# An attention and expert layer on eight cores: plain loads of V's weights, expert tiles started beside attention, expert rows stored by token

## The chip, the cores and the metric

The kernel runs on all 8 cores of one Trainium2 chip. Every core works on one of eight batch entries (2048 tokens of 1024 features) and holds its own copy of all weights; the cores exchange nothing. A core has TensorE (PE in the rows), VectorE (DVE), ScalarE (ACT), GpSimd (POOL) and SyncE (SP), and 16 DMA engines that all queues share. The metric is the device time in microseconds of the slowest core.

## What is computed

The reference, cut to what matters (x is one batch entry, B = 8, T = 2048, D = 1024):

```
xn = layernorm(x)
q, k, v = split(xn @ w_qkv.T + b_qkv)             # 16 heads of 64
q = silu(q);  k = softmax(k, over the tokens)
out = layernorm(q @ (k.T @ v)) * g + b            # per head: kv is 64x64
gate = sigmoid((xn @ w_g1.T + b_g1) @ w_g2.T + b_g2)
attn = (out * gate) @ w_out.T + b_out
logits = xn @ Wr.T                                # 8 experts
w = softmax(top_2(logits));  C = 769 rows at most per expert
ffn[t] = sum over the token's 2 experts of w[t,k] * (xn[t] @ We[expert])
y = x + attn + ffn
```

A token that arrives at a full expert is dropped there, and its row from that expert is zero. An expert gets 512 rows on average.

## The kernel before

All engines are programmed by hand: the code appends instructions to five lists (`PE`, `DV`, `AC`, `SP`, `GP`), each executed strictly in order, and `after` adds the semaphore waits. So what stands in a list behind a waiting instruction waits too. `move` appends a DMA to a list; `when` puts the instructions of a block between a branch and its target, on the engines named. Five weight slots of 2 MB in bfloat16 (`wring` 0 to 2 and the two halves of `wlate`) hold V's, K's, Q's, the eight experts' and the output weights one after another.

1. **Head** (`for s in range(NT + 2)`, line 484 on). Each of 16 tiles of 128 tokens is loaded from `x_tm` in float32, normalised (`h_stats`, `h_root`, `h_norm`), rounded to bfloat16 (`h_hi`), stored as `xn_d`, turned on TensorE into `xnT` (`h_trans`), multiplied by V's weights in two halves of 512 columns (`h_v`), and given to the router (`h_router`). V's weights arrive as two DMAs from GpSimd's queue that round from float32 on the way (`w_half`).
2. **K** (`for j in range(NJ + 2)`). 32 steps of projection, exponential, transpose and the product with V. The list `route` feeds the router's small VectorE work in beside them. At the start, nine stores of zeros clear the part of the expert results `eo_d` that experts may leave unwritten.
3. **Attention** (`for b in range(NB + 2)`, 8 units `u` each). Block b projects Q for 512 tokens (`q_proj`), block b+1 computes the attention rows and their statistics (`a_out`, `a_norm`), block b+2 the gate and the product (`a_gate`, `a_z`). So the last two blocks have no projection, and the last one has gates and products alone.
4. **Experts** (`for J in range(NJT)`, NJT = 40). Every expert has five tiles of 128 rows: four always, the fifth under a branch on the expert's count (`SURE` = 4). A sixth and seventh are under further branches (`m_rare`). Tile J: GpSimd gathers 128 rows of `xn_d` (`m_load`, six ahead), TensorE turns them and ScalarE copies them out (`m_trans`), 16 matmuls of 512 columns follow, VectorE scales one half by the token's weight and ScalarE the other (`m_rows`), and SP stores 256 KB to `eo_d`, ordered by expert and slot. Three buffers `eo` hold results on their way out. The branches stand on all five engines. GpSimd also loads the later weights by quarters (`next_quarter`), and SP the tiles of x for the last stage (`o_base`).
5. **Output** (`o_rows`, `o_proj`, `o_add`). For each of 16 token tiles GpSimd gathers the two expert rows of every token from `eo_d`, TensorE does 16 matmuls of the output projection and adds both gathered rows with four matmuls by the identity into the same banks, VectorE adds x and the bias, and ScalarE's queue stores y.

Lines to know: 298 is every matmul, 302 every transpose, 306 every activation, 313 ScalarE's and 314 VectorE's copies, 321 a tensor by a scalar, 317 a tensor by a tensor, 902 the gather of experts' rows, 1023 the gather of results, 112 and 120 branches.

## Time and profile before

| | us |
|---|---|
| three runs, median (lowest, highest) | 614.62 (614.15, 662.0) |
| the profiled execution, its own time | 614.46 |
| its span on the slowest core, core 0 | 612.9 |
| spans of the eight cores | 600.8 to 612.9 |
| head, to the first K projection | 0 to 118 |
| K | 118 to 222 |
| attention, blocks 0 to 3 | 222 to 313 |
| attention, blocks 4 and 5 | 313 to 350 |
| experts | 350 to 537 |
| output | 537 to 613 |

TensorE is busy for 486.9 us of the span (79%), VectorE for 267.4, ScalarE for 220.4 and GpSimd for 157.9. The chain that ended last is TensorE for 46% and DMA for 23%. The stages follow each other on TensorE, so an interval saved in one is saved at the end only if the next stage's inputs are there. A matmul row can be missing from the trace, so counts such as x15 in place of x16 mean nothing.

### The profile page before, as it was taken

Reading aid. Unit: us, or ns where it says so; the run is one execution under the profiler, and the core shown is the slowest. Engines: PE = TensorE matmul, PEld = TensorE weight load, DVE = VectorE, ACT = ScalarE, POOL = GpSimd, SP = SyncE. Lnnn points to the kernel's source line nnn. Section 1 sums busy time; section 2 is a strip of 40 time slices with the busy share of each in tenths; the row PEclk is TensorE's granted clock in tenths of the full one; section 3 lists DMA queues with packets and bytes.
Section 4 is the critical chain, followed back from the end, with each engine's and each line's share of the span. In section 5 each row is a group of like instructions: output and inputs, shape, how many; then the busy total and the mean of one; then the engine's idle time right before and its main releaser. Section 6 shows DMA issues by size and latency. Waiting matters only on the chain.

```text
span 612.9 us, 9186 instructions; the slowest of 8 cores (600.8 to 612.9 us)
## 1 busy us (share of the span) xinstructions
PE 486.9 (79%) x3080; PEld 247.7 (40%) x3136; DVE 267.4 (44%) x609; ACT 220.4 (36%) x339; POOL 157.9 (26%) x148
## 2 busy tenths in 40 slices
PE   0269999887679789997855598958778898899996
PEld 0135555444334454443422254424434444444442
DVE  1536766367885631465657611011110111315555
ACT  0414435253345423554543435334434354300000
POOL 3214445300090000100011425413322110055551
PEclk9979999999989989999965589999998998989999
DMA  9916991999990074000063349999999985158886
GB/s 162 223 52 193 194 249 55 169 221 211 214 185 15 1 110 65 0 1 2 0 90 49 103 124 207 254 225 193 215 173 198 215 264 157 69 153 235 247 240 240
DMA packets 40054, 91.54 MB, mean 149 GB/s; under 512 B 5632, under 2 KB 7808, under 8 KB 40000
## 3 DMA queue, kind: packets, MB, share of 16 engines
q0 software_dynamic: 21024, 44.39, 43.7%
q1 hardware_dynamic: 16528, 38.04, 18.8%
q10 hardware_dynamic: 2448, 8.42, 3.5%
q8 instruction: 30, 0.49, 0.4%
q14 instruction: 24, 0.20, 0.1%
HBM read 87.77 MB, written 28.57 MB: 190 GB/s over the span
## 4 chain that ended last, share of the span: by engine, by line
PE 46%; DMA 23%; DVE 12%; issue 11%; ACT 6%; DVEq 1%; POOL 0%; ACTq 0%; PEldq 0%; SPq 0%; POOLq 0%
PE PS L298 42%; DMA stage<-xn_d,tabs 9%; DMA eo_d<-stage 7%; DMA wr<-wv_t 5%; PE PS L302 4%; ACT stage L306 3%; DVE bst L816 3%; DVE nm L683 2%; DMA wlate<-x_tm 2%; ACT vq L306 1%; DVE stage L322 1%; ACT e_sb L313 1%; DVE nb L322 1%; DVE stage L317 1%; DVEq L100 0%
## 5 line engine op out<-in xcount | busy, mean ns | idle before, releaser
L298 PE MATMUL PS<-wr,xnt 128*128 128x512 bf16 x493 | 118.9, 391 | 17.0 <-DMA wr<-wv_t 9.4
L298 PE MATMUL PS<-xnt,wr 128*128 128x512 bf16 x492 | 118.4, 382 | 1.8 <-ACT vq L306 0.8
L321 DVE TENSOR_SCALAR stage<-PS,wslot_f 128x512 bf16<-128x512 f32 x36 | 26.9, 751 | 155.0 <-PE PS L298 111.7
L298 PEld LDWEIGHTS PS<-wr,xnt 128*128 128x128 bf16 x512 | 49.9, 100 | 77.7 <-issue 23.9
L302 PE MATMUL PS<-ident_sb,stage 128*128 128x128 bf16 x576 | 43.7, 226 | 46.9 <-DVE stage L314 21.9
L298 PE MATMUL PS<-wr,stage 128*128 128x512 bf16 x280 | 70.4, 405 | 5.3 <-ACT stage L313 4.2
L298 PEld LDWEIGHTS PS<-xnt,wr 128*128 128x128 bf16 x512 | 48.1, 98 | 50.4 <-issue 3.3
L298 PE MATMUL PS<-wlate,stage 128*128 128x512 bf16 x279 | 64.9, 381 | 1.2 <-ACT stage L313 0.8
L902 POOL DMA_INDIRECT stage<-xn_d,tabs x40 | 39.0, 974 | 94.8 <-PE PS L302 82.3
L302 PEld LDWEIGHTS PS<-ident_sb,stage 128*128 128x128 bf16 x576 | 37.8, 101 | 62.0 <-issue 52.8
L306 ACT ACTIVATE stage<-PS,wslot_f 128x512 bf16<-128x512 f32 x36 | 24.8, 688 | 83.6 <-PE PS L298 58.3
L1023 POOL DMA_INDIRECT stage<-eo_d,slot x32 | 35.1, 1096 | 63.8 <-DMA eo_d<-stage 37.7
L317 POOL TENSOR_TENSOR stage<-stage 128x1024 bf16<-128x1024 f32 x16 | 34.0, 2124 | 65.3 <-DVE stage L314 62.3
L298 PEld LDWEIGHTS PS<-wr,stage 128*128 128x128 bf16 x288 | 29.1, 104 | 39.8 <-issue 13.4
L313 ACT COPY stage<-PS 128x1024 bf16<-128x1024 bf16 x40 | 40.2, 1007 | 9.8 <-PE PS L302 9.7
L308 ACT ACTIVATE eT<-PS,nb 128x512 bf16<-128x512 f32 x32 | 22.0, 688 | 51.3 <-DVE nb L322 25.2
L298 PEld LDWEIGHTS PS<-wlate,stage 128*128 128x128 bf16 x288 | 27.6, 99 | 30.8 <-issue 1.5
L317 POOL TENSOR_TENSOR rs<-sd,half_sb 128x1 f32<-128x1 f32 x16 | 8.8, 549 | 108.6 <-DVE sd L321 108.6
L306 ACT ACTIVATE stage<-wlate,nmr,rs 128x1024 f32<-128x1024 f32 x16 | 19.8, 1240 | 41.2 <-DVE nmr L322 35.0
L326 DVE SCALAR_TENSOR_TENSOR xnt<-stage 128x512 bf16<-128x512 f32 x32 | 22.2, 693 | 20.2 <-ACT stage L306 16.6
L306 ACT ACTIVATE vq<-PS,nmr,rs 128x1024 bf16<-128x1024 f32 x16 | 19.3, 1204 | 30.9 <-DVE nmr L322 30.9
L683 DVE TENSOR_REDUCE nm<-PS 128x1 f32<-128x512 f32 x32 | 22.1, 690 | 16.0 <-PE PS L298 16.0
(138 smaller groups left out, 540.1 us busy)
## 6 DMA issues: line engine op xcount, KB each, us to landing
wlate<-x_tm SPq DMA_DIRECT2D x20, 512.0 KB, 6.6
eo_d<-stage SPq DMA_DIRECT2D x37, 256.0 KB, 8.5
eo_d<-stage SPq DMA_DIRECT2D x8, 768.0 KB, 37.1
wr<-we POOLq DMA_DIRECT2D x3, 2048.0 KB, 19.3
xn_d<-stage SPq DMA_DIRECT2D x16, 256.0 KB, 6.6
wlate<-we POOLq DMA_DIRECT2D x2, 2048.0 KB, 49.8
vq<-x_tm SPq DMA_DIRECT2D x8, 512.0 KB, 13.6
wlate<-we POOLq DMA_DIRECT2D x8, 512.0 KB, 24.1
```

What stands on the lines that cost most here:

```text
L298: return PE.run(lambda e: e.matmul(out, l, r, start=start, stop=stop), *toks, sig=sig)
L302: return PE.run(lambda e: e.transpose(out, in_, ident[:]), *toks, sig=sig)
L306: return AC.run(lambda e: e.activation(out, in_, func, bias=bias, scale=scale), *toks)
L308: return AC.run(lambda e: e.activation(out, in_, func, bias=bias, scale=scale, accum_out=acc), *toks)
L313: return AC.run(lambda e: e.copy(out, in_), *toks)
L317: return lane.run(lambda e: e.tensor_tensor(out, a, b, op), *toks)
L321: return lane.run(lambda e: e.tensor_scalar(out, a, s1, None, op0=op0), *toks)
L326: return lane.run(lambda e: e.scalar_tensor_tensor(out, a, s, b, op0=op0, op1=op1), *toks)
L683: a = DV.run(lambda e: e.tensor_reduce(nm[:, j:j + 1], bank[bk], AX.X, ALU.max, negate=True), p)
L816: m = DV.run(lambda e, h=h, bk=bk: e.bn_stats(bst[:, s, h, :], bank[bk]), p)
L902: GP.steps.append((lambda e: e.indirect_dma_start(out=out, out_offset=None, in_=xn_d, in_offset=bass.IndirectOffsetOnAxis(ap=tabs[:, col:c ...
L1023: GP.steps.append((lambda e: e.indirect_dma_start(out=dst, out_offset=None, in_=eo_d, in_offset=bass.IndirectOffsetOnAxis(ap=slot[:, col:c ...
```

## The change

- V's weights are loaded as float32 by plain DMAs, in eight pieces, from ScalarE's and SP's queues, and rounded by VectorE and ScalarE. The second half of the V product runs three tiles behind the first, so the head's loop has two steps more.
- The clearing of `eo_d` now covers the 4096 token rows (8 MB in place of 6.5), in four stores that are released in K's steps 20 to 23.
- A sixth weight slot lies in `stage`: expert 4's weights are loaded right after K, and from there each expert's weights, and the output weights, are loaded one expert earlier.
- Tiles 0 to 6 of the experts' 40 run in attention's blocks 4 and 5, one per two units (`m_beside`, `m_step`). Gathers run eight ahead in place of six, and there are six result buffers in place of three.
- GpSimd stores a tile's rows by token (row 2*token + choice of `eo_d`) with an indirect DMA (`m_put`) after each of all 40 tiles. Slots without a token go to spare rows.
- The output stage reads both rows of a token with one plain DMA of 512 KB per token tile from SP. One row is added on VectorE, the other by two matmuls with the identity.
- The branches stand on TensorE and VectorE alone (and on GpSimd for the sixth and seventh tile). ScalarE and SP have none.
- x's tiles for the output are loaded later, during experts 4 to 7, and their bias is added during experts 5 to 7 and before the output.

The diff, cut to its core:

```diff
-        wsl = [w[:] for w in wring] + [wlate[:, 0:HC * D], wlate[:, HC * D:2 * HC * D]]
+        wsl = [w[:] for w in wring] + [wlate[:, 0:HC * D], wlate[:, HC * D:2 * HC * D],
+                                       stage[:, 0:HC * D]]
...
-            x_tok = {0: load_x(0), 1: load_x(1)}
-            x_tok[2] = load_x(2, x_tok[0])
-            x_tok[3] = load_x(3, x_tok[1])
+            x_tok = {0: load_x(0)}
+            x_tok[1] = load_x(1, x_tok[0])
...
+            def wv_load(lane, h, q, *toks):
+                wv_in[h, q] = lane.move(
+                    counter(f"c_wv{h}{q}"), wvf[h][:, 2 * q:2 * q + 2, :],
+                    wv_t.rearrange("(c p) o -> p c o", p=128)[:, 2 * q:2 * q + 2,
+                                                              512 * h:512 * (h + 1)], *toks)
+            def wv_cast(lane, h, c):
+                t_wv[h, c] = tcopy(lane, wv3[0][:, c, 512 * h:512 * (h + 1)], wvf[h][:, c, :],
+                                   wv_in[h, c // 2])
+            for q in range(4):
+                wv_load(AC, 0, q)
+            act(warm[:], eps_sb[:], AF.Sqrt, t_const)
+            x_tok[2] = load_x(2, wv_in[0, 3])
+            wv_load(SP, 1, 0)
+            wv_load(SP, 1, 1)
+            x_tok[3] = load_x(3)
+            wv_load(SP, 1, 2)
+            wv_load(SP, 1, 3)
...
+                    late["wk"] = w_load(1, wk_t, stat[t], *[t_wv[1, c] for c in range(HC)])
...
-            for s in range(NT + 2):
+            wv_cast(AC, 0, 3)
+            for s in range(NT + 4):
...
+                if s in (2, 3):
+                    for c in range(4 * s - 8, 4 * s - 4):
+                        wv_cast(AC, 1, c)
...
+                v0 = h_v(s - 1, 0) if 1 <= s <= NT else None
+                v1 = h_v(s - 4, 1) if s >= 4 else None
...
+                b = ts(DV, idle[:], tok_f[:], 0.0, ALU.is_lt, None, None, a)
+                a = tt(DV, tok_i, tok_f[:], idle[:], ALU.add, b)
+                tk["tab"] = DV.run(lambda e: e.tensor_single_scalar(
+                    tabs[:], tok_i, 1, ALU.arith_shift_right), a)
+                b = tt(DV, idle[:], idle[:], spare[:], ALU.mult, a)
+                tk["dst"] = tt(DV, dtab[:], tok_f[:], idle[:], ALU.add, b)
...
-            wslot = {e: (3, 4, 0, 1, 2)[e % 5] for e in range(E)}
+            wslot = {e: (3, 4, 0, 1, 5, 2)[e % 6] for e in range(E)}
...
-            for e in range(E):
-                t_ez = SP.move(
-                    c_ez, eo_d[e * SE + 128 * SURE:(e + 1) * SE, :].rearrange(
-                        "(k p) d -> p k d", p=128),
-                    nil.rearrange("p (o d) -> p o d", o=1).broadcast_to([128, ET - SURE, D]),
-                    t_nil, stat[NT - 1])
-            t_ez = SP.move(c_ez, eo_d[NSLOT:NSLOT + 128, :], nil)
+            def clear_rows():
+                for q in range(4):
+                    tk["clear"] = SP.move(
+                        c_ez, eo_d[q * T // 2:(q + 1) * T // 2, :].rearrange(
+                            "(k p) d -> p k d", p=128),
+                        nil.rearrange("p (o d) -> p o d", o=1).broadcast_to([128, 8, D]),
+                        t_nil, kv_pe[20 + q])
...
+            load_we(4, 5, tk["hot_free"])
...
+            def a_pair(t):
+                return t % 2 if t < NT - 4 else 0
...
+            BESIDE = 7
...
+            def m_load(J):
+                xg_tok[J] = fetch_rows(c_xg[J % 8], xg[J % 8], (J // XE) * ET + J % XE, tk["tab"],
+                                       xtr.get(J - 8), ao_pe[NT - 5 if J % 8 < 4 else NT - 1],
+                                       *[xd_tok[t] for t in range(NT - 4, NT)])
...
+            def put_rows(done, src, col, *toks):
+                GP.after(*toks)
+                GP.steps.append((lambda e: e.indirect_dma_start(
+                    out=eo_d, out_offset=bass.IndirectOffsetOnAxis(ap=dtab[:, col:col + 1], axis=0),
+                    in_=src, in_offset=None), done, 16))
+                return done.up(16)
...
+                    if h == 0 or i >= SURE:
+                        a = ts(DV, half, bank[bk], w, ALU.mult, None, None, p, tk["tw"], *free)
+                    else:
+                        a = act(half, bank[bk], AF.Copy, p, tk["tw"], *free, scale=w)
...
+            def m_out(J):
+                pair = 1 if J < 3 else J % 2 if J < BESIDE else J % 3
+                mo_pe[J], out_tok[J] = m_rows(J // XE, J % XE, pair, xgT[J % 3], xgt_tok[J],
+                                              eo[J % 6], [st_tok.get(J - 6), ntr[NB - 2] if
+                                                          2 <= J < 6 else None, t_ez])
+            def m_put(J):
+                st_tok[J] = put_rows(c_eo[J % 6], eo[J % 6], (J // XE) * ET + J % XE, tk["dst"],
+                                     t_ez, *out_tok[J])
...
+            def m_step(J):
+                e, i = J // XE, J % XE
+                if J + 1 < NJT:
+                    m_trans(J + 1)
+                if i < SURE:
+                    m_out(J)
+                else:
+                    with where(e, 128 * SURE, PE, DV):
+                        m_out(J)
+                        pair = (J + 1) % 2 if J < BESIDE else (J + 1) % 3
+                        with where(e, 128 * (SURE + 1), PE, DV, GP):
+                            m_rare(e, SURE + 1, pair)
+                            with where(e, 128 * (SURE + 2), PE, DV, GP):
+                                m_rare(e, SURE + 2, pair)
+                    freed[e] = PE.now()
+                    if e + 6 < E:
+                        t_we[e + 6] = quarters(wslot[e], we[e + 6:e + 7, :, :].rearrange(
+                            "e a b -> (e a) b"), freed[e])
+                    elif e + 6 == E:
+                        wo["slot"] = wslot[e]
+                        wo["tok"] = quarters(wslot[e], wo_t, freed[e])
+                m_put(J)
+                if J + 8 < NJT:
+                    m_load(J + 8)
+                next_quarter()
+                for k in range(4):
+                    if J // XE == 4 + k and i < 4:
+                        o_base(4 * k + i, freed[3 + k])
+                    if J // XE == 5 + k and i < 4:
+                        o_bias(4 * k + i)
+            def m_beside(b, u):
+                if b == 0 and u == 0:
+                    for lane in (PE, DV, GP):
+                        lane.after(tk["cnt"])
+                        lane.read(cnt_i)
+                if b == 0 and u == 7:
+                    for J in range(4, 8):
+                        m_load(J)
+                if b == 0 and u == 1:
+                    m_trans(0)
+                if u % 2 and b * 8 + u >= 3:
+                    m_step((b * 8 + u - 3) // 2)
...
+                    if b >= NB:
+                        m_beside(b - NB, u)
                 if b == NB - 1:
-                    load_we(4, 2, qfree[NB - 1])
+                    for J in range(4):
+                        m_load(J)
+                    t_we[5] = quarters(2, we[5:6, :, :].rearrange("e a b -> (e a) b"),
+                                       qfree[NB - 1])
+                    next_quarter()
+                    next_quarter()
...
-                return p, SP.move(done, eo_d[e * SE + 128 * i:e * SE + 128 * (i + 1), :], out, a, b)
...
+            for J in range(BESIDE, NJT):
+                m_step(J)
...
-                ga[t] = gather(c_ga[i], ga_sb[i], t, t_rows, tk["si"], t_ez, rows_pe.get(t - 4),
-                               *t_st)
-                gb[t] = gather(c_gb[i], gb_sb[i], NT + t)
...
+                r_tok[t] = SP.move(c_rows[t % 4], rows_sb[t % 4], eo_d[256 * t:256 * (t + 1), :]
+                                   .rearrange("(p k) d -> p (k d)", k=2),
+                                   rows_pe.get(t - 4), r0_tok.get(t - 4), *t_st)
...
-                for k, (rows, got) in enumerate(((ga_sb[s], ga[t]), (gb_sb[s], gb[t]))):
-                    for h in range(2):
-                        p = mm(bank[2 * s + h], ident[:], rows[:, 512 * h:512 * (h + 1)], False,
-                               k == 1, got, sig=(k == 1))
+                r0_tok[t] = tt(DV, xb[t], rows_sb[s][:, 0:D], xb[t], ALU.add, r_tok[t], xo_tok[t])
+                for h in range(2):
+                    p = mm(bank[2 * s + h], ident[:],
+                           rows_sb[s][:, D + 512 * h:D + 512 * (h + 1)], False, True, r_tok[t],
+                           sig=(h == 1))
                 rows_pe[t] = p
-                a = tt(DV, xb[t], PS[:, 1024 * s:1024 * (s + 1)], xb[t], ALU.add,
-                       p, xo_tok[t])
+                a = tt(DV, xb[t], PS[:, 1024 * s:1024 * (s + 1)], xb[t], ALU.add, p, r0_tok[t])
...
+            for t in range(NT - 4, NT):
+                o_bias(t)
```

The order on TensorE in attention's block 4, one pair of units, before (gate: `gh,wg_sb`; turned attention rows: `ident_sb,vq`; attention product: `kv_sb,vq`):

```order
250 L298 MATMUL PS<-kv_sb,vq 128x128 x8
251 L298 MATMUL PS<-gh,wg_sb 128x512
252 L302 MATMUL PS<-ident_sb,vq 128x128 x4
253 L298 MATMUL PS<-gh,wg_sb 128x512
254 L302 MATMUL PS<-ident_sb,vq 128x128 x4
```

and the same place now, a pair later (the transposes x12 are four of attention and eight of the next expert tile):

```order
256 L310 MATMUL PS<-gh,wg_sb 128x512
257 L314 MATMUL PS<-ident_sb,vq 128x128 x4
258 L310 MATMUL PS<-kv_sb,vq 128x128 x8
259 L310 MATMUL PS<-gh,wg_sb 128x512
260 L314 MATMUL PS<-ident_sb,vq 128x128 x12
261 L310 MATMUL PS<-wlate,stage 128x512 x16
262 L310 MATMUL PS<-gh,wg_sb 128x512
```

A tile's 16 matmuls now stand between two gates, so the next gate and all that waits for it come behind them.

The order on ScalarE in blocks 4 and 5, before (`vq<-PS,nmr,rs`: the attention rows normalised; `stage<-PS,bg_sb`: the gate):

```order
183 L306 ACTIVATE vq<-PS,nmr,rs 128x1024
184 L306 ACTIVATE stage<-PS,bg_sb 128x512 x2
185 L306 ACTIVATE vq<-PS,nmr,rs 128x1024
186 L306 ACTIVATE stage<-PS,bg_sb 128x512 x2
187 L306 ACTIVATE vq<-PS,nmr,rs 128x1024
```

and now:

```order
187 L318 ACTIVATE stage<-PS,bg_sb 128x512 x2
188 L318 ACTIVATE vq<-PS,nmr,rs 128x1024
189 L325 COPY stage<-PS 128x1024
190 L318 ACTIVATE stage<-PS,wslot_f 128x512
191 L318 ACTIVATE stage<-PS,bg_sb 128x512 x2
192 L318 ACTIVATE vq<-PS,nmr,rs 128x1024
```

Between the normalisation and the next two gates stand a copy (the next tile turned) and half a tile's scaling.

GpSimd at the end of expert 0 and the start of expert 1's rows, before (`xn_d` is the gather, `we` a quarter of a weight; the branches belong to the sixth and seventh tile):

```order
33 L902 DMA stage<-xn_d,tabs 128x1024
34 L105 UNCONDITIONAL_BRANCH x3
35 L100 UNCONDITIONAL_BRANCH
36 L902 DMA stage<-xn_d,tabs 128x1024
37 L75 DMA wlate<-we 128x2x1024
```

and now:

```order
55 L108 UNCONDITIONAL_BRANCH
56 L111 UNCONDITIONAL_BRANCH
57 L965 DMA eo_d<-vq,dtab 11264x1024
58 L940 DMA vq<-xn_d,tabs 128x1024
59 L78 DMA wlate<-we 128x2x1024
```

The store of results has moved from SP's queue to GpSimd's, where it stands ahead of the next gather and quarter.

## Rows read from the trace of the kernel before

**Rows 1.** windows by stage: each engine's busy us (instructions), granted clock, DMA share, GB/s.

```profile
0.00:118.00 118.00, 81.36 (x756) 48.02 (x771) 59.63 (x139) 40.12 (x65) 44.88 (x37) 0.97 0.72 161
...
313.00:350.00 37.00, 20.98 (x111) 10.15 (x108) 25.10 (x52) 16.11 (x21) 8.41 (x10) 0.50 0.54 96
350.00:537.00 187.00, 153.11 (x882) 77.38 (x899) 31.15 (x42) 76.57 (x88) 45.10 (x50) 0.94 0.84 188
537.00:613.00 76.00, 70.29 (x314) 31.46 (x318) 34.69 (x30) 0.00 (x0) 35.08 (x32) 0.97 0.74 225
```

**Rows 2.** timeline, head: start us, us, engine, line, operation, tile, count, idle before.

```profile
24.76 3.57 PE L298 MATMUL PS<-wr,xnt 128*128 128x512 bf16 x8 [1.88 <-DMA wr<-wv_t]
...
35.83 3.37 PE L298 MATMUL PS<-wr,xnt 128*128 128x512 bf16 x8 [7.50 <-DMA wr<-wv_t]
```

**Rows 3.** chain of waits in the head: start us, us, what.

```profile
100.75 0.89 PE PS L302 x16
...
105.87 0.89 PE PS L302 x16
```

**Rows 4.** timeline, attention's last two blocks.

```profile
325.80 1.20 ACT L306 ACTIVATE vq<-PS,nmr,rs 128x1024 bf16<-128x1024 f32 x1 [2.65 <-DVE nmr L322]
...
331.74 1.20 ACT L306 ACTIVATE vq<-PS,nmr,rs 128x1024 bf16<-128x1024 f32 x1 [2.65 <-DVE nmr L322]
...
346.55 0.69 ACT L306 ACTIVATE stage<-PS,bg_sb 128x512 f32<-128x512 f32 x1 [0.88 <-PE PS L298]
...
348.12 0.69 ACT L306 ACTIVATE stage<-PS,bg_sb 128x512 f32<-128x512 f32 x1 [0.88 <-PE PS L298]
```

**Rows 5.** timeline, experts' tiles, ScalarE and TensorE.

```profile
491.61 0.61 PE L302 MATMUL PS<-ident_sb,stage 128*128 128x128 bf16 x8 [0.75 <-PEq L112]
...
503.31 0.61 PE L302 MATMUL PS<-ident_sb,stage 128*128 128x128 bf16 x8
503.63 0.69 ACT L306 ACTIVATE stage<-PS,wslot_f 128x512 bf16<-128x512 f32 x1 [2.31 <-PE PS L298]
...
504.21 1.00 ACT L313 COPY stage<-PS 128x1024 bf16<-128x1024 bf16 x1
...
507.21 0.61 PE L302 MATMUL PS<-ident_sb,stage 128*128 128x128 bf16 x8
...
513.62 1.01 PE L302 MATMUL PS<-ident_sb,stage 128*128 128x128 bf16 x8 [2.35 <-ACTq L112]
```

**Rows 6.** waits of TensorE in the experts: us in total, times, longest.

```profile
PE PS L302 <- DMA stage<-xn_d,tabs: 13.4, 8, 4.1
PE PS L302 <- ACTq L112: 7.8, 4, 2.4
PE PS L298 <- ACT stage L313: 4.9, 3, 2.3
PE PS L298 <- ACTq L112: 3.2, 2, 2.4
```

**Rows 7.** DMA issues in the experts: count, KB each, median us to landing.

```profile
eo_d<-stage SPq DMA_DIRECT2D x36, 256.0 KB, 8.4
...
stage<-xn_d,tabs POOLq DMA_INDIRECT x34, 20.3
```

**Rows 8.** loads and stores of xn_d, issue to landing.

```profile
DMA to landing us min/median/max: 2.0/10.1/33.8
```

**Rows 9.** DMA queues, 218 to 243 us, one weight load: packets, MB, share.

```profile
q0 software_dynamic: 1040, 2.10, 61.2%
```

**Rows 10.** DMA queues, 341 to 354 us, six gathers.

```profile
q0 software_dynamic: 480, 1.57, 46.9%
```

**Rows 11.** DMA queues, 512 to 533 us, plain stores and loads.

```profile
q1 hardware_dynamic: 940, 2.21, 31.0%
```

**Rows 12.** timeline, output stage.

```profile
601.40 3.62 PE L298 MATMUL PS<-wr,xnt 128*128 128x512 bf16 x15
601.74 1.23 DVE L317 TENSOR_TENSOR wlate<-PS,wlate 128x1024 f32<-128x1024 f32 x1 [1.96 <-PE PS L298]
```

357 lines of the change are left out of this document (161 added, 196 removed).

## The prediction, made before the changed kernel ran

> **What bounds the kernel now.** I read the windows by stage first, to see which stage is full and which is not. In the output stage TensorE is busy for 70.3 of 76 us, in the experts for 153.1 of 187, and in attention's last two blocks for 21.0 of 37 at a granted clock of 0.50, the lower level of 1.2 GHz [rows 1]. The first is bound by TensorE's work, the other two by something else.
>
> Then the timelines, for the distance between equal events. A full tile of the head costs 5.12 us (100.75 to 105.87, [rows 3]), back to back, so the head is TensorE's once V's weights are there; they are late: the first half ends a wait at 24.76 us and the second at 35.83 [rows 2]. In block 4 one normalisation follows another after 5.94 us, in block 5 one gate another after 1.57 us [rows 4]. An undisturbed expert tile costs 3.90 us (503.31 to 507.21, [rows 5]), 16 matmuls of 512 columns and eight transposes. A wide matmul takes about 0.22 us there (70.3 us for 314 in the output, [rows 1]). Then the waits of TensorE in the experts: 13.4 us for gathered rows, 4.9 for ScalarE's copy of them, and 11.0 (7.8 + 3.2) for ScalarE's sequencer at a branch [rows 6]; one such wait is 2.35 us, where TensorE's own branch costs 0.75 [rows 5]. So the experts lose time to transfers and to branches of another engine.
>
> **The change, part by part.** All times are against the profiled execution (614.46 us, span 612.9), which stands 0.2 us from the median of the three runs.
>
> Head: until the pipeline can run with both halves (step 4) five tiles of x and all of V's weights must land, 2.6 + 4.2 MB. At full share the head's DMAs moved 161 / 0.72 = 224 GB/s [rows 1]: 30 us. The nearest plain transfers took 31.0% of 21 us for 2.21 MB, 2.9 us per MB [rows 11]: 20 us. I take 30, since all 16 engines also wait for memory there. Done by then are three half products (3 x 1.7 us) and some 3 us of transposes and routing; left are 16 x 5.12 - 8 = 74 us. The first K projection comes at 104 instead of 118: **-14**. Bounds: -20 (second half usable at 24), -6 (at 38). The 16 roundings lie beside it: VectorE is busy for 60 and ScalarE for 40 of 118 us [rows 1].
>
> K and blocks 0 to 3: five small VectorE operations fewer, more zeros later and one weight earlier, where no DMA ends a wait of TensorE: **0**. The zeros must only land before block 2 writes over their source.
>
> Blocks 4 and 5: the loop of 5.94 us runs through VectorE's statistics, GpSimd's power, ScalarE's normalisation and the next gate. ScalarE now has a copy of 1.00 and a scaling of 0.69 us [rows 5] between the normalisation and that gate: 5.94 + 1.69 + 0.2 for two more starts = 7.8, three times, and once the copy alone: +6.6. In block 5 a pair of gates takes 3.14. Now the tile's 3.90, then its scaling 0.69, a gate's activation 0.69, and about 1.0 for the second gate, its transposes and the handovers, follow each other on TensorE: 6.3, four times: +12.6. I add 1 for matmuls that still start at the lower clock: **+20** for seven tiles that cost 27.3 at least where they stood. The eight register reads move with their cost. GpSimd has a store, a gather and a quarter per step, about 1 us each, in a step of 6.3 to 7.8, and the power is asked for behind them; if they take over 4 us, the next statistics wait.
>
> Experts: before, 350 to 537 less the register reads, about 184 us, for 36 computed tiles (36 x 3.90 = 140) and 44 of loss. After, 29 computed tiles are left on this core: 113. Four skipped ones cost a turn and a branch, 1.2 each: 5. Seven branches on TensorE at 0.75: 5. ScalarE's 11.0 go. The DMA's demand from the end of block 3 is four weights at 61.2% of 25 us = 15.3 [rows 9], 40 gathers at 46.9% of 13 us / 6 = 1.0 [rows 10], 40 stores, and 16 tiles of x at 1.5 (0.52 MB by [rows 11]). A store by index isn't in the trace. As a plain store it is 0.77 [rows 11]; as a gather 1.0 (I take this one, it is the same queue and the same number of rows); at worst one row packet as slow as under the weights' load, 15.3 / 2 MB x 0.26 = 1.9. Sum: 61 + 41 + 41 + 24 = 167 us in the 185 until the experts end (203 with the worst). While the quarters run, five tiles ask for 4 x 3.8 + 5 x 2.0 = 25 us in 20.5, so a backlog of about 10 to 15 us builds up. That is less than the lead of the gathers (eight tiles, 31 us) and of the buffers (six, 23 us). I leave 6 us for what slips through. 113 + 5 + 5 + 6 = 129, against 184: **-55**. Bounds: -61 (no waits left), -35 (the worst store, DMA bound at 203).
>
> Output: 32 matmuls by the identity go, 32 x 0.22 = 7.0. TensorE stays the bound: VectorE has two additions of 1.23 us [rows 12] in a tile of 3.9 us. DMA moves 1.05 MB per tile, 270 GB/s, where it now moves 225 at share 0.74 [rows 1]. The first rows wait for the last store by index; three projections (10.4 us) cover it: 1 us late. **-6**.
>
> Sum: -14 + 20 - 55 - 6 = -55, so 614.5 becomes **559**.
>
> **One rule against the change.** Stores from SP's queue landed after 8.4 us in the experts, the gathers of GpSimd's queue after 20.3 in the same stretch [rows 7]. The Trainium skill, DMA: Bandwidth & Descriptors, section Queues, rings and completion order, says that each DMA engine takes turns between the queue rows it has work for, while a row's own descriptors are consumed in order. By that rule a result store that leaves SP's row queues behind every weight quarter and gather, whatever its own price; the trace agrees (20.3 against 8.4). By bytes alone the sum would keep 8.4 us and no risk; by the rule the landing is 20 us and more, and the six buffers are needed. Rival 3 is what it gives at worst.
>
> **The rivals.** (1) As forecast: 0.62. Its own range is 543 to 573, from the bounds of head and experts.
>
> (2) The tiles beside attention run at the lower clock. For: it stood at 0.50 all through blocks 4 and 5 [rows 1]. Against: 3.5 us of wide matmuls in a step of 6.3 to 7.8 is a new kind of work there, and the experts' mean is 0.94 with 18% of idle time [rows 1]. Seven tiles at half speed cost 3.45 more each: +24, 583. Chance 0.12.
>
> (3) Slower than before: result stores land too late. A tile may write its buffer when the store six tiles back has landed. With a landing time L a tile then costs (L + 1) / 6 us, which decides from L = 22.4 on. The 20.3 is a median; the slowest gather took 33.8 [rows 8]. If 33 steps went at L = 33.8, a tile would cost 5.8 instead of 3.9: +63, 622. From L = 32 on the whole gain is gone. Against: the output weights are loaded by tile 17, and the plain stores leave SP's queue, so congestion covers half the stage. Chance 0.06.
>
> (4) The same shortage in a mild form: stores at the worst price and L near 26, +0.6 us per tile or the DMA bound of 203: +16 to +20, 575 to 579. Chance 0.14.
>
> (5) Nearly all expert waits vanish and V's weights come in 20 us: 541 to 545. Chance 0.06.
>
> **How the numbers follow.** The likeliest case gives 559. The range of 8 in 10 reaches from 540 (just under case 5) to 592 (cases 2 and 4 with some of the bounds on top), and leaves out case 3 and the sums of several mishaps. Within 2% of the time before, about what a measurement of this kernel tells from no change, is 602 to 627: cases 2 and 4 together, or case 3 in part, 0.06. Slower by more than 2%, the rest of case 3: 0.05. Faster by over 2%: 0.89.
>
> **What would show it.** Right: the first K projection near 104 us, ScalarE without table loads between experts' tiles, steps of about 7.8 us in block 4 and 6.3 in block 5 with the clock at its upper level, tiles of 3.90 us afterwards with under 10 us of waits for DMAs, and an output stage with tiles of 3.9 us. Wrong: the second half's first product after 38 us; steps over 9 us beside attention, with idle time ended by GpSimd or a gather; VectorE or ScalarE waiting for the stores of `eo_d` (the buffers); or TensorE waiting for rows of `eo_d` in the output.

## The result: faster by 4.6%, about half of what was forecast

The changed kernel took 0.954 of the time of the kernel before (95% interval 0.947 to 0.962). Its profiled execution took 586.6 us (span 584.9, core 0), against 614.5 (span 612.9). The forecast was 559 us, within 540 to 592; so the range held, but the likeliest case did not come. In a later comparison the same kernel stood at 0.951 (0.945 to 0.958). In some executions the cores of one die run several per cent slower, whatever the kernel, and all comparisons here leave those out.

The windows of the changed kernel, core 0, cut at its own stages (columns as in [rows 1]): head, K, blocks 0 to 3, blocks 4 and 5 with the seven tiles beside them, the other 33 expert steps, output:

```profile
0.00:112.00 112.00, 83.23 (x768) 48.87 (x769) 63.77 (x145) 46.25 (x77) 41.73 (x34) 0.95 0.76 191
112.00:217.00 105.00, 84.36 (x578) 44.41 (x577) 71.97 (x240) 43.62 (x107) 17.59 (x7) 0.93 0.73 150
217.00:307.00 90.00, 80.31 (x468) 37.34 (x466) 44.76 (x108) 44.44 (x60) 8.81 (x15) 1.00 0.31 50
307.00:367.00 60.00, 40.37 (x240) 20.82 (x240) 28.51 (x56) 25.35 (x32) 26.42 (x27) 0.77 0.53 121
367.00:514.00 147.00, 129.41 (x765) 65.27 (x764) 41.70 (x50) 50.02 (x61) 68.50 (x72) 0.94 0.84 207
514.00:585.00 71.00, 62.32 (x288) 28.11 (x288) 42.44 (x36) 0.00 (x0) 1.76 (x1) 0.97 0.71 241
```

| stage, core 0 | forecast change | measured change |
|---|---|---|
| head, to the first K projection | -14 | -6 |
| K and blocks 0 to 3 | 0 | 0 |
| blocks 4 and 5, now with seven tiles | +20 | +23 |
| experts | -55 | -40 |
| output | -6 | -5 |
| sum | -55 | -28 |

Two terms carry most of the miss of 27 us: 8 us in the head, 15 in the experts. The waits of TensorE in the experts of the changed kernel (367 to 520 us) answer to [rows 6]:

```profile
PE PS L314 <- DMA vq<-xn_d,tabs: 11.2, 3, 4.8
PE PS L314 <- DVEq L115: 2.4, 2, 1.2
PE PS L310 <- DVEq L115: 1.2, 1, 1.2
PE PS L310 <- ACT stage L325: 1.1, 2, 0.6
```

ScalarE's sequencer is gone from the list. The gathers cost nearly as much as before (13.4), but in three waits close together. The timeline of TensorE shows them; tiles before and behind this stretch are 3.90 us apart:

```profile
423.66 3.62 PE L310 MATMUL PS<-stage 128*128 128x512 bf16 x16
427.11 0.61 PE L314 MATMUL PS<-ident_sb,vq 128*128 128x128 bf16 x8
427.56 3.62 PE L310 MATMUL PS<-stage 128*128 128x512 bf16 x16
435.19 1.01 PE L314 MATMUL PS<-ident_sb,vq 128*128 128x128 bf16 x8 [4.02 <-DMA vq<-xn_d,tabs]
436.00 6.03 PE L310 MATMUL PS<-stage 128*128 128x512 bf16 x16
444.41 1.01 PE L314 MATMUL PS<-ident_sb,vq 128*128 128x128 bf16 x8 [2.37 <-DMA vq<-xn_d,tabs]
450.20 1.01 PE L314 MATMUL PS<-ident_sb,vq 128*128 128x128 bf16 x8 [4.78 <-DMA vq<-xn_d,tabs]
451.00 5.37 PE L310 MATMUL PS<-wr,stage 128*128 128x512 bf16 x16
456.65 3.62 PE L310 MATMUL PS<-wr,stage 128*128 128x512 bf16 x16
```

From 427.56 to 456.65 there are 29.1 us, where three steps of 3.90 and a skipped tile (the transposes at 444.41, without a product) take 13.6 in an undisturbed stretch. The 15.5 us between them are the experts' whole miss. Some 4 us of it are two groups of matmuls at a lower granted clock (6.03 and 5.37 us instead of 3.62) behind the waits. All three waits of TensorE name a gather. VectorE waits there too, for a free buffer, that is for a result store six tiles back:

```profile
441.52 0.75 DVE L333 TENSOR_SCALAR vq<-PS,wslot_f 128x512 bf16<-128x512 f32 x1 [9.13 <-DMA eo_d<-vq,dtab]
```

Windows of the same kernel around the stall:

```profile
370.00:380.00 10.00, 9.60 (x63) 4.95 (x60) 2.06 (x3) 3.87 (x6) 5.54 (x6) 1.00 0.69 137
380.00:430.00 50.00, 47.03 (x292) 24.19 (x293) 9.01 (x12) 19.87 (x24) 32.97 (x35) 1.00 1.03 212
430.00:455.00 25.00, 13.83 (x57) 6.38 (x56) 1.70 (x3) 4.41 (x5) 6.86 (x7) 0.66 1.01 264
455.00:514.00 59.00, 55.95 (x335) 27.98 (x333) 26.90 (x30) 20.18 (x25) 20.51 (x21) 1.00 0.64 195
```

The next-to-last column is what to read: the DMA engines are full from 380 to 455 us, and at 0.64 afterwards. The stall comes at the end of a full stretch, not at its beginning.

The first of the three waits can be followed from its gather, the one of tile 24 (tiles counted from 0; the row is GpSimd issuing it):

```profile
412.70 0.97 POOL L940 DMA_INDIRECT vq<-xn_d,tabs  x1 [0.30 <-issue]
```

TensorE was free for these rows at 431.17, 18.5 us later, and got them at 435.19. The changed kernel issues a gather eight tiles ahead, but that is not a lead of eight tiles: gather J+8 stands behind the store of tile J in GpSimd's list, and its transposes stand ahead of the matmuls of tile J+7 in TensorE's. Six tiles lie between. In an undisturbed stretch that is 21.3 us (the gather of tile 35 leaves at 467.08, its transposes start at 488.41: six tiles and a branch, less 3 us in which tile J is scaled and stored), and less where one of the six tiles is skipped, as here.

### The profile page after: what moved, and what is told of

Read it like the earlier page. It is cut to its first block, busy times and chain, and to the rows that moved or that the text cites. A ratio compares the mean times of both kernels' runs of the same rounds, so it can differ in the third digit from the quotient of the medians.

```text
span 584.9 us, 9174 instructions; the slowest of 8 cores (568.9 to 584.9 us)
## 1 busy us (share of the span) xinstructions
PE 480.0 (82%) x3104; PEld 244.8 (42%) x3104; DVE 293.1 (50%) x634; ACT 209.7 (36%) x337; POOL 164.8 (28%) x154
## 4 chain that ended last, share of the span: by engine, by line
PE 56%; DMA 13%; DVE 12%; issue 9%; ACT 6%; DVEq 1%; POOL 1%; ACTq 0%; SPq 0%; POOLq 0%; PEldq 0%
PE PS L310 51%; DMA vq<-xn_d,tabs 6%; PE PS L314 5%; DMA wlate<-x_tm 5%; DVE nm L735 3%; DMA wr<-wv_t 2%; ACT stage L318 2%; DVE bst L875 2%; ACT vq L318 1%; DVE stage L334 1%; ACT ek L325 1%; DVE nb L334 1%; DVE stage L329 1%; ACT stage L325 1%; DVE wlate L329 1%
## 5 line engine op out<-in xcount | busy, mean ns | idle before, releaser
L314 PE MATMUL PS<-ident_sb,vq 128*128 128x128 bf16 x448 | 40.4, 234 | 25.3 <-DMA vq<-xn_d,tabs 15.0
L333 DVE TENSOR_SCALAR vq<-PS,wslot_f 128x512 bf16<-128x512 f32 x28 | 21.0, 751 | 78.5 <-PE PS L310 69.3
L310 PE MATMUL PS<-wr,stage 128*128 128x512 bf16 x224 | 52.4, 388 | 0.6 <-ACT stage L325 0.6
L314 PEld LDWEIGHTS PS<-ident_sb,vq 128*128 128x128 bf16 x448 | 30.4, 104 | 43.1 <-issue 37.2
L940 POOL DMA_INDIRECT vq<-xn_d,tabs x40 | 40.3, 1008 | 12.2 <-issue 11.3
L965 POOL DMA_INDIRECT eo_d<-vq,dtab x26 | 27.9, 1073 | 55.5 <-ACT vq L318 31.2
L320 ACT ACTIVATE ek<-PS,nb 128x512 bf16<-128x512 f32 x32 | 22.0, 687 | 50.6 <-DVE nb L334 26.0
L314 PE MATMUL PS<-ident_sb,stage 128*128 128x128 bf16 x256 | 18.5, 229 | 17.9 <-DVE stage L326 13.8
L310 PEld LDWEIGHTS PS<-wr,stage 128*128 128x128 bf16 x224 | 21.8, 100 | 25.2 <-issue 2.9
L318 ACT ACTIVATE vq<-PS,wslot_f 128x512 bf16<-128x512 f32 x20 | 13.8, 688 | 51.0 <-PE PS L310 51.0
```

The source lines that it names most:

```text
L310: return PE.run(lambda e: e.matmul(out, l, r, start=start, stop=stop), *toks, sig=sig)
L314: return PE.run(lambda e: e.transpose(out, in_, ident[:]), *toks, sig=sig)
L318: return AC.run(lambda e: e.activation(out, in_, func, bias=bias, scale=scale), *toks)
L320: return AC.run(lambda e: e.activation(out, in_, func, bias=bias, scale=scale, accum_out=acc), *toks)
L333: return lane.run(lambda e: e.tensor_scalar(out, a, s1, None, op0=op0), *toks)
L940: GP.steps.append((lambda e: e.indirect_dma_start(out=out, out_offset=None, in_=xn_d, in_offset=bass.IndirectOffsetOnAxis(ap=tabs[:, col:c ...
```

## Experiments: the stall in the experts

All ratios are to the kernel before, on the same chip in the same comparison. There were four such groups on four chips, and the anchor is in the first one only (with the next three kernels), so ratios of different groups are compared by their intervals. Times within a kernel are from the profile of core 0 unless another core is named. One core's span varies from execution to execution (core 0 of the anchor: 576.4 to 584.0 us), so the main measure of the stall here is the time that TensorE waits for gathers behind 360 us, as the mean of the eight cores of the profiled execution. It is 8.1 us in the anchor (9.4 on core 0).

**The anchor.** Nothing is edited.

> The changed kernel as it is, as the anchor of the experiments on the same chip. Every theory expects a ratio of 0.947 to 0.962 to the kernel before, about 587 us in the profiled run, with one stretch near 420 to 455 us in which TensorE waits about 16 us for gathers and buffers, and expert tiles of 3.90 us before it.

Measured: 0.951 (0.945 to 0.958), profiled 587.9 us. The DMA issues of its core 0 from 415 to 450 us (count, KB each, median us to landing):

```profile
wr<-x_tm SPq DMA_DIRECT2D x4, 512.0 KB, 15.3
stage<-x_tm SPq DMA_DIRECT2D x4, 512.0 KB, 14.2
wr<-wo_t POOLq DMA_DIRECT2D x2, 512.0 KB, 27.3
vq<-xn_d,tabs POOLq DMA_INDIRECT x9, 27.0
eo_d<-vq,dtab POOLq DMA_INDIRECT x5, 26.4
eo_d<-stage,dtab POOLq DMA_INDIRECT x3, 26.7
```

The prediction had a limit: a store that lands later than 22.4 us after its issue holds its buffer too long. Here the stores take 26.4. All that GpSimd issued, weights, gathers and stores, landed alike after 26 to 27 us, and SyncE's loads after 14 to 15. The Trainium skill, DMA: Bandwidth & Descriptors, section Queues, rings and completion order, says that the engines take turns between queue rows and consume one row in order; by that rule the trace agrees (26.4 to 27.3 us in one row, 14.2 to 15.3 in the other).

**First theory (A): bursts of x.** With its stores gone, nothing paces SyncE's loads of x; four leave at once at 418 and 445 us.

```diff
-                        o_base(4 * k + i, freed[3 + k])
+                        o_base(4 * k + i, freed[3 + k], mo_pe[J])
```

> Each of the 16 loads of x waits for the last matmul of the tile in whose step it is issued, instead of leaving SyncE's queue in a burst of four. Theory A (the bursts of four x loads, which nothing on SyncE's queue holds back any more, collide with the quarters of the output weights and delay gathers and stores): the stall near 420 to 455 us shrinks from 16 to under 4 us, the kernel gains 12 to 16 us on the changed kernel, 571 to 575. Theory B (GpSimd's queue itself has too much to carry: gathers, stores by index and the quarters of the output weights): under 4 us of gain, the stall stays. Theory C (the lower granted clock is the cause and the waits follow from it): under 4 us, and the granted clock falls before the first wait.

Measured: 0.953 (0.947 to 0.959). TensorE's two waits for gathers are 5.5 and 6.9 us, at 439 and 447; the mean of the cores is 7.5 us. Theory A fell. Theory C fell by the windows of the changed kernel: its first wait begins at 431.17, the granted clock (third column from the end) is 1.00 before it and 0.50 only behind it:

```profile
428.00:431.00 3.00, 3.00 (x15) 1.26 (x13) 0.00 (x0) 1.02 (x2) 1.80 (x2) 1.00 1.01 223
435.00:437.00 2.00, 1.80 (x11) 1.28 (x12) 0.00 (x0) 0.70 (x1) 0.50 (x1) 0.50 1.04 285
```

**The output weights a little later.**

```diff
-                next_quarter()
+                if J < 14 or J % 2 == 0:
+                    next_quarter()
```

> From expert tile 14 on GpSimd issues a quarter of weights only at every second tile, so the output weights are spread over tiles 14 to 20 instead of 14 to 17. Theory A: the x bursts still come in one piece, now on top of the quarters themselves; the stall stays or moves, gain within 4 us. Theory B: the backlog on GpSimd's queue is gone, gain 8 to 14 us. Theory C: no change.

Measured: 0.957 (0.951 to 0.963). The stall split and moved: TensorE waits 4.6 us for a gather at 438 and 8.9 us at 462 (mean of the cores 8.0), and the gain of 8 to 14 us that theory B had did not come. The last quarter leaves at tile 20 instead of 17, still inside the full stretch.

**Stores out of GpSimd's queue.**

```diff
-                st_tok[J] = put_rows(c_eo[J % 6], eo[J % 6], ..., tk["dst"], t_ez, *out_tok[J])
+                st_tok[J] = SP.move(c_eo[J % 6], eo_d[128 * (J % 32):128 * (J % 32) + 128, :],
+                                    eo[J % 6], t_ez, *out_tok[J])
```

> Results of the expert tiles are stored plainly from SyncE's queue to 128 consecutive rows, as before the change, so they are not at their tokens' rows (the output is computed from other rows; the amount of work in the output stage is the same). The loads of x stand behind those stores on SyncE again and are paced by them. Theory A: the same gain as with paced loads of x, 12 to 16 us, no more than 3 us beyond it. Theory B: 12 to 20 us, at least 5 us more than paced loads of x alone, since 40 stores leave GpSimd's queue. In attention's last two blocks GpSimd's power comes sooner: steps there shorten by 0.3 to 0.6 us each, 2 to 4 us in all.

Measured: 0.941 (0.934 to 0.947), profiled 575.5 us; the median is 9 us under the anchor's, short of the 12 that both theories had at least. This kernel leaves out the order of rows by token, so it does not compute the reference's result. On core 0 no gather is waited for behind 360 us (mean of the cores 0.4). One stall of 9 to 10 us is left, and it is another: VectorE stands 17.7 us at its first addition of the bias, because x has not landed, and everything behind it on VectorE stands too:

```profile
452.40 1.23 DVE L329 TENSOR_TENSOR wr<-wr,bv_sb 128x1024 f32<-128x1024 f32 x1 [17.65 <-DMA wr<-x_tm]
```

GpSimd's busy time from 367 to 514 us falls from 69 to 29 us (34 stores by index, three gathers and three quarters fewer stand in that window): a store by index holds GpSimd for 1.0 us. The steps in block 4 shorten from 7.9 to 7.5 us (means of the cores). So the queue matters, but the bytes were still late for somebody. That asks for a theory of the engines as a whole (D).

**x later.**

```diff
-                    if J // XE == 4 + k and i < 4:
-                        o_base(4 * k + i, freed[3 + k])
+                if J >= 24:
+                    o_base(J - 24, freed[3 + (J - 24) // 4], mo_pe[J])
...
```

The additions of the bias move behind the loads with them.

> Pacing the loads of x or spreading the output weights a little gave nothing, so a new pair of theories. D: the 16 DMA engines themselves are full from about 380 to 455 us (share 1.01 to 1.06 in every 10 us), because four weights, the gathers, the stores and x all fall into the same stretch, and any byte in it costs. B2: only the order on GpSimd's queue matters. Here the loads of x are issued one per tile from tile 24 on, about 8 tiles (8 x 1.6 = 13 us of the engines) later than before, while GpSimd's queue is untouched. D: the stall near 425 to 455 us shrinks by 8 to 14 us and the kernel gains 6 to 13 us on the changed kernel (573 to 580). B2: under 3 us of gain (x is in SyncE's queue).

Measured: 0.948 (0.942 to 0.955), profiled 580.1 us. On core 0 one gather is waited for behind 360 us, 4.2 us; the mean of the cores is 2.2 us instead of 8.1. From 415 to 450 us its stores land after 9.7 to 12.4 us:

```profile
wr<-x_tm SPq DMA_DIRECT2D x4, 512.0 KB, 6.4
vq<-xn_d,tabs POOLq DMA_INDIRECT x9, 10.4
eo_d<-vq,dtab POOLq DMA_INDIRECT x6, 12.4
eo_d<-stage,dtab POOLq DMA_INDIRECT x3, 9.7
```

GpSimd's queue was not touched, and yet what it carries lands in less than half the time and is waited for less: by the waits and landings B2 fell and D stands. The kernel's time does not tell them apart. The ratio is only 0.003 under the anchor's, 2 us, with intervals that overlap, where D had 6 to 13 us and B2 under 3. Core 0's span was 567.0 us in this profile (584.0 in the anchor's), but 565.4 to 579.1 over the four executions compared; the mean over all cores and those executions is 571.6 us against 576.4. The slowest core gained less: core 7 still waits 6.2 us for gathers behind 360 us.

**The output weights much later.**

```diff
-                next_quarter()
+                if J < 14 or (J >= 25 and J % 2):
+                    next_quarter()
```

> The four quarters of the output weights are issued at tiles 25, 27, 29 and 31 instead of 14 to 17; x is loaded as in the changed kernel. D and B2: both take about 8 to 10 us of the engines out of the full stretch and out of GpSimd's queue: gain 6 to 12 us on the changed kernel (574 to 580). If this gains and later loads of x do not, it is B2; if both gain about alike, D. If neither gains, the stall is something else.

Measured: 0.943 (0.938 to 0.947), some 5 us under the anchor, with intervals that just overlap. Core 0: 567.8 us, and TensorE waits for no gather behind 360 us (mean of the cores 1.1). In the waits both kinds of deferral work alike, as D has it.

**Gathers by index against plain loads from the same queue.**

```diff
-                GP.steps.append((lambda e: e.indirect_dma_start(out=out, ..., in_=xn_d, ...), done, 16))
-                return done.up(16)
+                at = 128 * (col % NT)
+                return GP.move(done, out, xn_d[at:at + 128, :], *toks)
```

> The gathers of token rows are plain loads of 128 consecutive rows from the same queue (other rows are computed; the number of tiles, stores by index, weights and x is the same). The page of the changed kernel shows the packets of the gathers to take about 1.7 us of all engines per tile, where the prediction counted 1.0. Theory D with the gather as the mis-sized term: a tile's demand falls by about 1 us (34 us for the tiles from block 4 on), the full stretch and the stall disappear (every tile 3.9 us), gain 14 to 18 us on the changed kernel: 569 to 573. If it is the stores by index that are dear, the stall stays and the gain is under 5 us.

Measured: 0.926 (0.921 to 0.932), profiled 573.5 us, the gain that D expected, some 15 us. This kernel too computes other results, since it leaves out the choice of rows. Behind 360 us TensorE waits once for rows, 2.3 us (mean of the cores 2.2). A part of the gain lies earlier: between 300 and 360 us the mean wait for gathers falls from 5.6 to 1.9 us. Its windows:

```profile
380.00:430.00 50.00, 45.03 (x283) 23.38 (x286) 9.01 (x12) 19.98 (x25) 25.21 (x33) 1.00 1.03 253
430.00:455.00 25.00, 24.10 (x145) 12.25 (x147) 10.92 (x12) 9.32 (x12) 8.71 (x13) 1.00 0.89 288
```

At the same share of 1.03 the engines move 253 GB/s instead of 212 in this stretch. The expectation's size of the term was wrong, though: it named a difference of about 1 us per gather. From 300 to 515 us GpSimd's queue takes 62.4% in the anchor and 54.5% here, for 29.10 and 29.37 MB; 7.9% of 215 us is 17 us, or 0.42 us for each of 40 gathers:

```profile
q0 software_dynamic: 10672, 29.10, 62.4%
```

```profile
q0 software_dynamic: 10752, 29.37, 54.5%
```

So 17 us of DMA time less, spread over these 215 us, were enough to end the stall.

**Without tiles beside attention.**

```diff
-            BESIDE = 7
+            BESIDE = 0
...
-                if u % 2 and b * 8 + u >= 3:
-                    m_step((b * 8 + u - 3) // 2)
```

> No expert tile runs beside attention's last two blocks: all 40 follow them; nothing else is changed. By the prediction's terms the tiles beside attention cost 20 us there and save 27.3 us of experts' time, so without them the kernel is 7 us slower than the changed kernel (593). If the experts are bound by the DMA engines from tile 7 on anyway, the tiles that run earlier only bring the full stretch forward, and the loss is 0 to 5 us, or there is a gain where the steps beside attention cost more (they took 22.6 us): 583 to 592.

Measured: 0.963 (0.958 to 0.968), 591.5 us: by the ratios 7 us slower than the anchor, give or take 5, which agrees with the prediction's terms. The gathers are waited for 14.8 us on core 0 (mean of the cores 11.3), so the stall is there too.

**ScalarE's branches restored.**

```diff
-                    if h == 0 or i >= SURE:
+                    if h == 0:
...
-                    with where(e, 128 * SURE, PE, DV):
+                    with where(e, 128 * SURE, PE, DV, AC):
```

> The branches on ScalarE are back (half of a conditional tile's scaling and the branch itself), with the register reads before attention's last two blocks. The prediction counted 11 us of TensorE's waits for ScalarE's sequencer. If they are on the path, the kernel is 6 to 11 us slower than the changed kernel (593 to 598). If the experts are bound by the DMA engines, TensorE's waits for the branch come off the stall: 0 to 4 us slower up to tile 25, and 1 to 1.5 us for each of the three branches after it: 588 to 592.

Measured: 0.960 (0.956 to 0.964), 591.2 us: by the ratios 5 us slower than the anchor, give or take 5, where the prediction had counted 11. With the branches 11 table loads of 1.28 us each are back on ScalarE between 350 and 511 us; the changed kernel has none there. The waits for gathers do not shrink in return (mean of the cores 8.7 us, 8.1 in the anchor).

## Experiments: the head

The mark used here is the first reduction of K on VectorE, 1.8 to 2.0 us behind the first K projection. Before, after, and with the old loads, on core 0:

```profile
119.73 0.69 DVE L683 TENSOR_REDUCE nm<-PS 128x1 f32<-128x512 f32 x1 [2.34 <-PE PS L298]
```

```profile
114.00 0.69 DVE L735 TENSOR_REDUCE nm<-PS 128x1 f32<-128x512 f32 x1 [7.03 <-PE PS L310]
```

```profile
107.72 0.69 DVE L735 TENSOR_REDUCE nm<-PS 128x1 f32<-128x512 f32 x1 [7.03 <-PE PS L310]
```

The cores of one execution differ in this mark by 1.4 to 6 us, so a single core does not price a part of the change. The start of the same row on all eight cores, in the profiled executions:

| kernel | core 0 | mean of eight | lowest to highest |
|---|---|---|---|
| before | 119.7 | 119.7 | 117.6 to 120.7 |
| changed | 114.0 | 112.7 | 111.1 to 114.0 |
| anchor (the same kernel) | 115.0 | 113.0 | 111.1 to 115.0 |
| old loads | 107.7 | 107.3 | 106.6 to 108.0 |
| old loads and old order | 113.2 | 114.1 | 113.0 to 115.1 |
| reordered head | 115.8 | 113.7 | 110.7 to 116.7 |
| ScalarE's queue | 111.8 | 112.2 | 110.6 to 113.2 |

**V's old loads, everything else changed.** The roundings are gone, and x tiles 1 to 3 are issued at the start.

```diff
-            for q in range(4):
-                wv_load(AC, 0, q)
+            for h in range(2):
+                a = GP.move(c_w[0] if h == 0 else counter("c_wb"), wv3[0][:, :, 512 * h:512 * (h + 1)], ...)
```

> V's weights are loaded by GpSimd's casting transfers in two halves as before the change, with x tiles 1 to 3 issued as before; the order of the products in the head and everything else are the changed kernel's. This prices the first part of the change alone. The prediction has it at 14 us (599 here). The trace of the changed kernel has the first K projection only 6 us earlier than before: then 5 to 7 us slower than the changed kernel, 591 to 593.

Measured: the expectation had the wrong sign. With the old loads the mark comes *earlier* than in the changed kernel, by 6.3 us on core 0 and by 5.7 on the mean of the cores against the anchor. TensorE waits longer for V's first half, which landed at 21.7 us (the row names a small cast of VectorE that ended just then), and then not again:

```profile
21.97 3.19 PE L310 MATMUL PS<-wr,xnt 128*128 128x512 bf16 x8 [9.68 <-DVE io_f L326]
26.56 1.89 PE L310 MATMUL PS<-wr,xnt 128*128 128x512 bf16 x8 [0.50 <-DVE xnt L326]
```

In the changed kernel the first product starts at 17.63, but the next ones wait for VectorE, which itself had waited until 20.99 us for x's third tile:

```profile
17.63 3.56 PE L310 MATMUL PS<-wr,xnt 128*128 128x512 bf16 x8 [2.81 <-DVE xnt L326]
25.24 1.86 PE L314 MATMUL PS<-ident_sb,stage 128*128 128x128 bf16 x16 [4.05 <-DVE wr_hl L326]
30.85 3.57 PE L310 MATMUL PS<-wr,xnt 128*128 128x512 bf16 x8 [3.75 <-DVE xnt L326]
```

Behind these waits lie the landings. V was there as a whole at 32.4 us in the changed kernel and at 31.5 with the old loads, so the plain loads brought only its first half sooner (16.1 instead of 21.7). And x's fifth tile landed at 33.7 us instead of 20.7.

The kernel's ratio is 0.947 (0.941 to 0.953), not told apart from the anchor's. On core 0 TensorE now waits 12.9 us for gathers behind 360 us instead of 9.4 to 11.2, as if the experts had taken the head's gain back; but the mean of the cores is 7.9 us, no more than the anchor's 8.1. The spans of the eight cores are 575.3 us on the mean in this profile and 578.9 in the anchor's. How much of the head's gain reaches the end is open.

**Old loads and V's second half in its old place.**

```diff
-                v1 = h_v(s - 4, 1) if s >= 4 else None
+                v1 = h_v(s - 1, 1) if 1 <= s <= NT else None
```

> V's old casting loads as in the run before, and the products with the second half of V back in the step of the first half (before the change they were there; the changed kernel has them three steps later). If the later second half is what made the head faster (TensorE waited 7.5 us for it before), the first K projection comes at 113 to 117 instead of 107.7. If the lighter start (tables made on chip, x tile 0 first) did it, it stays at 107 to 109. The kernel: within 5 us of the changed kernel with old loads either way.

Measured: mark at 113.2 on core 0 and 114.1 on the mean; kernel 0.960 (0.956 to 0.965). TensorE waits 5.4 us for the second half. So, by the means, the three steps' delay of the second half is worth 6.8 us, what is left of the change in the head (tables made on chip, fewer early transfers; not tried apart) the 5.6 us from 119.7 to 114.1, and the plain loads with their roundings cost 5.7.

**Why the plain loads cost: order or weight.** Two kernels; the first puts x tile 2 ahead of V's second half and VectorE's normalisation ahead of the next statistics for four steps, the second puts all of V into ScalarE's queue and leaves x alone in SyncE's.

```diff
+            x_tok[2] = load_x(2, x_tok[1])
...
+                if s + 1 < NT and s < 4:
+                    h_norm(s + 1)
```

> Head only: x tile 2 is issued right behind tile 1, ahead of V's second half, and in the first four steps VectorE does the next tile's normalisation factors before the statistics of the tile after it. Old casting loads made the first K projection come at 107.7 us instead of 112.2, so the plain loads of V cost time. Theory H (x tiles 2 and 3 stand behind V's weights and VectorE's order makes each tile wait for them): the first K projection comes at 105 to 108. Theory W (V's 16 roundings and the weights themselves are what is late): it stays at 110 to 112. In either case the kernel's time changes by less than 4 us, because the experts' full stretch at the DMA engines gives the head's gain back, as it did with the old loads (stall of 19 us instead of 16).

```diff
+            x_tok[2] = load_x(2, x_tok[0])
+            x_tok[3] = load_x(3, x_tok[1])
...
+            for q in range(4):
+                wv_load(AC, 1, q)
```

> V's weights are still loaded plainly and rounded on chip, but all eight transfers are in ScalarE's queue, and x tiles 1 to 3 are issued at the start as before the change, alone in SyncE's queue. Theory Q (the x tiles stood behind V's second half in SyncE's queue: one issued at 19 us landed at 34.6 in the run with the reordered head): TensorE no longer waits over 3 us for an x tile after its first, and the first K projection comes at 106 to 109 us instead of 112. Theory W (4 MB of weights at once are late in whatever queue, or the 16 roundings hold VectorE and ScalarE): 111 to 115. The kernel's time: within 3 us of the changed kernel in both, since the experts give a head's gain back.

(The first of these expectations sets 107.7, a mark, against 112.2, a first K projection; mark against mark it is 107.7 and 114.0.)

Measured: marks at 113.7 and 112.2 on the mean, kernels at 0.952 (0.947 to 0.956) and, without a ratio, at 588.1 and 588.7 us in two executions. Neither order brings 107 on any core, and neither differs from the anchor's 113.0 by more than the cores do among themselves. In the second, where x has a queue to itself, VectorE stands 3.7 and 2.1 us at roundings of V, whose weights have not landed, with the next x tile's work behind them:

```profile
10.00 0.43 DVE L326 CAST wr<-wr 128x512 bf16<-128x512 f32 x1 [3.74 <-DMA wr<-wv_t]
19.42 0.43 DVE L326 CAST wr<-wr 128x512 bf16<-128x512 f32 x1 [2.08 <-DMA wr<-wv_t]
```

Theory Q fell, and so did theory H. In the second kernel x's fifth tile landed at 27.1 us and V as a whole at 32.0. That the roundings on an in-order engine tie x's chain to V's landing fits these rows; it was not tried apart from the weights' own transfer time, so their shares stay open.

## Versions meant to beat both

The first keeps V's old loads, spreads the 12 quarters of the last three weights over tiles 4 to 22, and loads x from tile 24 on; the second spreads the quarters to tile 26 and the loads of x over tiles 27 to 39 (`X_AT` lists which in which step).

```diff
+                if J < 2 or (J >= 4 and J % 5 in (0, 2, 4)):
+                    next_quarter()
```

> A version meant to beat both: V's old casting loads with the late second half, the 12 quarters of the last three weights spread over tiles 4 to 22 (three in five tiles) instead of three bursts of four, and x one tile per step from tile 24 on. By theory D the demand is then about 2.5 us (gather and store) + 1.4 (quarters) or + 1.6 (x) in a tile of 3.9, so the stall of 16 to 20 us goes and the head's 4.5 us are kept: 19 to 22 us less than the changed kernel, 563 to 568. If the engines have no slack left later, 570 to 575.

Measured: 0.939 (0.934 to 0.943), 579.2 us at the median: 8 us less than the anchor by the ratios, where the forecasts were 19 to 22, or 570 to 575 us. Behind 360 us core 0 waits once for a gather (3.9 us, mean of the cores 2.4); mean of the cores 569.8 us, but cores 6 and 7 need 578.8 and 581.0.

```diff
+                if J < 2 or (J >= 4 and J % 2 == 0):
+                    next_quarter()
+                for t in X_AT.get(J, ()):
+                    o_base(t, freed[3 + t // 4], mo_pe[J])
```

> As the version with even demand (old casting loads of V, quarters spread, x late), but smoother: one quarter at every second tile from 4 to 26, x only from tile 27 on (16 loads in tiles 27 to 39, two at some after the gathers end at 31), and the addition of the bias for 12 tiles in the output stage. In the other version two cores still waited 4 to 5 us for a gather near tile 29, where x and the quarters' backlog met. Expected: no such wait; 3 to 6 us less than that version, 572 to 576, if VectorE with three additions of 1.2 us in an output tile of 3.9 us does not become the bound.

Measured: 0.934 (0.927 to 0.941), 577.2 us at the median, the lowest ratio of the kernels that compute the reference's result, 1.8% under the anchor's 0.951, with intervals that do not touch. It is not told apart from the version before it (0.939). Core 0 waits for no gather behind 360 us (mean of the cores 0.4), and its windows there stay under a share of 1:

```profile
380.00:430.00 50.00, 47.31 (x292) 24.45 (x296) 9.66 (x14) 19.73 (x24) 31.44 (x34) 1.00 0.92 208
430.00:455.00 25.00, 23.22 (x146) 12.01 (x147) 5.16 (x7) 9.98 (x12) 16.03 (x18) 1.00 0.92 208
455.00:494.00 39.00, 37.16 (x216) 18.57 (x218) 11.95 (x15) 12.94 (x17) 12.04 (x13) 1.00 0.96 297
```

A third version (old loads, output weights late, x paced at its old places) was forecast at 0.935 to 0.940 and came to 0.936 (0.929 to 0.944).

One wait for a gather is in all three still, near 347 us and thus in block 5: 7.5 us on core 0 of the second version, 7.2 on the mean of its cores (3.8 us on core 0 of the changed kernel, 5.2 on the mean). It belongs to tile 4, whose gather leaves GpSimd at the end of block 4 (at 340.97 in the changed kernel) and is wanted 4.4 us later. None of the three issues it earlier in the list.

## Why the prediction was off by half

**Head (-14 forecast, -6 measured): the step that failed is the start of the full loop at 30 us.** It said that by then all five x tiles and V could have landed and that the 16 roundings "lie beside it", from VectorE's 60 busy of 118 us. V landed at 32.4 and the fifth x tile at 33.7 us, and the loop with both halves began at 40.7 (34.4 with the old loads, 3 us behind V). A mean share says little of an engine that works in order at the start: VectorE stood at roundings and at late x tiles, and everything behind them stood too. How much of the delay is the roundings' and how much the weights' own transfer is open. The forecast also priced the head in one sum, by the landing of V; the runs give +12 us to the later second half and the rest of the change, and -6 to the plain loads.

**K, blocks 0 to 3 (0) and output (-6): right**, 0 and -5. **Blocks 4 and 5 (+20, measured +23): right in mechanism.** The steps of block 4 are 8.2 us apart on core 0 (7.9 on the mean of the cores) where 7.8 was forecast, and a wait that it did not count, for the gather of tile 4, takes 3.8 us:

```profile
320.68 1.29 DVE L875 BATCH_NORM_STATS2 bst<-PS 128x6 f32<-128x512 f32 x2
...
328.91 1.29 DVE L875 BATCH_NORM_STATS2 bst<-PS 128x6 f32<-128x512 f32 x2
```

The granted clock there went from 0.50 to 0.77, and matmuls of a tile took 3.6 to 5.3 us, so rival 2 did not come. The run without these tiles agrees with the net 7 us of the two terms (7 measured, give or take 5).

**Experts (-55 forecast, -40 measured): the step that failed is the comparison of the backlog with the lead.** The sum of the engines' demand was about right (167 us forecast; 62.4% + 12.4% of 215 us is 161 in the anchor), and so was the tile of 3.90. But it set "a backlog of about 10 to 15 us" against a lead of the gathers of "eight tiles, 31 us", and left 6 us for what slips through. The lead is six tiles: 21.3 us measured, and 18.5 where a skipped tile lies between. The backlog was too small as well: 25 us asked for in 20.5 leave 4.5 us behind per burst of quarters, so three bursts make up the forecast's figure, and x, which stood in the sum of the stage, is not in it. In the kernel three bursts of quarters and two of x leave between 362 and 447 us, the engines are full for 75 us, and gathers land after 22.5 us at the first wait and 27.0 at the median of the stretch. The stores reached 26.4 us, past the 22.4 that the prediction had worked out itself for the buffers; VectorE waits for them, but TensorE's own waits all name gathers. This comes near rival 4, "L near 26", with its +16 to +20 against +15 measured; it was given a chance of 0.14. The form was another: one stall within three tiles, not 0.6 us in each. The rule of the Trainium skill that stood beside it, and by which the landing would be "20 us and more", was the better guide than the bytes. That a longer lead of the gathers would end the stall was not tried; what was tried is less to carry. Two prices were off besides. The gather's was read in a quiet stretch [rows 10], and over 300 to 515 us it costs 0.4 us more than a plain load of as many rows. And ScalarE's 11 us of sequencer waits were worth about 5; where the rest went is open.

**What a single part is worth.** The old loads bring K 5.7 us earlier, and the kernel's ratio moves by 0.004, within its interval; reordering the head moved the kernel by nothing that can be measured. So the parts' gains cannot be added up from these runs.
